# Lots behind the counts: one-hots as the stationary operand, rows as two exact 12-bit parts

## The reference

```
h = relu(layernorm(x))
x = x + sum over edges e into dst of  h[src_e] @ W0[etype_e]^T  + b0
h = relu(layernorm(x))
x = x + leaky_relu( sum over edges of norm_e * (h @ W1)[src_e] + b1, 0.2 )   # norm_e from the degrees
```

## Time and profile before

| | us |
|---|---|
| median of 3 runs | 2731.56 (2728.19 to 2732.8) |
| the profiled execution | 2727.95 |
| its span, first to last instruction | 2726.2 |
| mean granted TensorE clock | 0.903 |
| busy: PE, PEld, DVE, ACT, POOL | 2162.9, 1906.5, 1258.2, 1603.4, 1618.0 |

### The profile page before, as it was taken

How to read it: one execution, slowest core, us unless ns; L and a number is a source line. 1 busy time by engine, 2 the same in 40 slices (tenths; PEclk the granted TensorE clock), 3 DMA queues, 4 the chain that set the end, 5 groups by cost and what they waited for, 6 DMA issues and landing times.

```text
span 2726.2 us, 45144 instructions
## 1 busy us (share of the span) xinstructions
PE 2162.9 (79%) x14621; PEld 1906.5 (70%) x14621; DVE 1258.2 (46%) x3564; ACT 1603.4 (59%) x3885; POOL 1618.0 (59%) x1719
## 2 busy tenths in 40 slices
PE   1557777787787778767868889899898888898898
PEld 1446666776677677766757778787777777777776
DVE  6436545555564655555555542222222223344258
ACT  6425655666575667647656775656566656556450
POOL 2666666556665665565655556666666666666615
PEclk7678888888898898888989999999999999989899
DMA  9334444444554454445555456454445444555448
GB/s 287 104 92 121 131 118 144 123 126 129 148 162 139 124 157 132 125 122 147 153 159 157 128 149 202 142 167 135 141 126 148 132 132 127 128 137 129 123 92 107
DMA packets 366992, 378.04 MB, mean 139 GB/s; under 512 B 238627, under 2 KB 288036, under 8 KB 366628
## 3 DMA queue, kind: packets, MB, share of 16 engines
q0 software_dynamic: 85312, 221.42, 29.5%
q1 hardware_dynamic: 236772, 110.05, 15.0%
q10 hardware_dynamic: 44672, 43.64, 4.8%
HBM read 299.78 MB, written 75.19 MB: 138 GB/s over the span
## 4 chain that ended last, share of the span: by engine, by line
PE 58%; issue 13%; another core or an unknown queue 9%; DVE 9%; ACT 8%; ACTq 1%; DVEq 1%; DMA 0%; SPq 0%
PE ps_slot L1670 22%; PE ps_slot L1732 10%; PE ps_proj L1686 10%; PE ps_aux L1732 8%; PE ps_slot L1700 6%; ACT staged_f L1311 3%; ACT gap_f L1376 2%; DVE hots_f L1560 2%; DVE hots_f L1557 1%; ACT onehot_f L1384 1%; DVE acc_f L1462 1%; ACT wide_f L1369 1%; PE ps_aux L1809 1%; DVE acc_f L1600 1%
## 5 line engine op out<-in xcount | busy, mean ns | idle before, releaser
L1132 POOL DMA_INDIRECT rows_f<-table,idxT x1612 | 1531.3, 950 | 958.8 <-issue 394.6
L1670 PE MATMUL ps_slot<-onehot_f,rows_f 128*128 128x128 f32 x6448 | 952.5, 297 | 161.0 <-issue 97.5
L1670 PEld LDWEIGHTS ps_slot<-onehot_f,rows_f 128*128 128x128 f32 x6448 | 885.1, 209 | 203.3 <-issue 153.7
L1311 ACT ACTIVATE staged_f<-ps_slot 128x392 uint8<-128x392 f32 x784 | 343.8, 493 | 439.8 <-remote 270.9
L1376 ACT ACTIVATE gap_f<-iota,keyT 128x128 bf16<-128x128 bf16 x1614 | 526.8, 393 | 67.0 <-ACT staged_f L1311 33.6
L1557 DVE TENSOR_TENSOR hots_f<-ps_slot,keys_f 128x392 bf16<-128x392 bf16 x784 | 279.4, 356 | 557.7 <-remote 337.1
L1700 PE MATMUL ps_slot<-hots_f 128*128 128x98 bf16 x3136 | 246.9, 219 | 235.0 <-issue 103.4
L1384 ACT ACTIVATE onehot_f<-gap_f 128x384 f32<-128x384 bf16 x538 | 276.3, 514 | 220.0 <-remote 160.2
L1686 PE MATMUL ps_proj<-w0t,acc_f 128*128 128x256 f32 x1568 | 382.5, 393 | 25.2 <-issue 22.6
L1700 PEld LDWEIGHTS ps_slot<-hots_f 128*128 128x128 bf16 x3136 | 198.8, 117 | 284.3 <-issue 235.6
L1462 DVE TENSOR_TENSOR acc_f<-ps_slot,acc_f 128x256 f32 x538 | 227.5, 423 | 327.2 <-remote 185.5
(11 more groups left out here) (166 smaller groups left out, 970.2 us busy)
## 6 DMA issues: line engine op xcount, KB each, us to landing
rows_f<-table,idxT POOLq DMA_INDIRECT x1612
abuf_f<-counts_d SPq DMA_DIRECT2D x57, 320.0 KB
stash_f<-table SPq DMA_DIRECT2D x14, 1280.0 KB
table<-hs_f SPq DMA_DIRECT2D x48, 256.0 KB
xt_f<-in_x_dram SPq DMA_DIRECT2D x48, 128.0 KB
out_dram<-xt_f SPq DMA_DIRECT2D x48, 128.0 KB
xres<-in_x_dram SPq DMA_DIRECT2D x9, 640.0 KB, 14.0
table<-xres SPq DMA_DIRECT2D x9, 640.0 KB, 6.0
```

What stands on the lines that cost most here:

```text
L1132: eng.indirect_dma_start(rows0[:, k, c, :], None, V["table0"], bass.IndirectOffsetOnAxis(ap=idxT[:, n * LOT + c:n * LOT + c + 1], axis=0)) ...
L1311: eng.activation(staging[:, h % 2, :, (w % HSUB) * SUB:(w % HSUB + 1) * SUB], count_bank(w)[:, 0:SPAN * MW].rearrange("p (d t) -> p t d", ...
L1670: last = eng.matmul(o[:, b * W:(b + 1) * W], rows0[:, k, c, b * P:(b + 1) * P], onehot[:, n % HOTS, c, :], start=(c == 0), stop=(c == chun ...
```

## The change

For lots 322 to 530 (segments 29 to 47, the lots that start after the counts are over and stop before the last segment) the product is turned round. The one-hots are the weights, and the gathered rows move, 256 columns at a time, in f32r. To keep that exact the rows are split: DVE writes a rounded copy (`high_part`) into one of 2 new buffers, and the difference over the row itself (`low_part`). PE does 6 matmuls a lot (`sum_turned`) into banks 2 and 0 in turn; ACT copies the sums of a fill to SBUF (`take_sums`), PE turns them back with 2 fp32 transposes a lot (`turn_sums`) into bank 1, and DVE accumulates from there, one slot later than before. The planner books 0.9 us instead of 1.3 us for such a lot, the projections and chains from tile 30 on stand one slot later, and the scratch memory for gather descriptors is 8192 bytes.

```
+TURNED_FROM = 29
+HIGHS = 2
...
-        return base + (1 if t >= LATE_TILE else 3), base + (3 if t >= LATE_TILE else 7)
+        return base + (2 if t >= LATE_TILE else 3), base + (4 if t >= LATE_TILE else 7)
...
+        stored[-2] -= 2
...
-                pe += 1.3 + 0.28 * len(self.win.get(n - LEAD, ())) + (3.45 if n in self.project else 0.0)
+                pe += (0.9 if self.turned[0] <= n < self.turned[1] else 1.3) + 0.28 * len(self.win.get(n - LEAD, ())) + (3.45 if n in self.project else 0.0)
...
+            def take_sums(f):
+                until = lots_until(f)
+                width = (until - first_lot(f)) * DF
+                eng.wait_ge(s_pe, until)
+                if f >= F1 + 2:
+                    eng.wait_ge(s_turn, f - 1 - F1)
+                eng.activation(summed[:, f % 2, 0:width], ps_slot[:, SUM_BANKS[(f - F1) % 2], 0:width], ACT.Copy).then_inc(s_sum, 1)
...
             def accumulate(n, off):
-                eng.wait_ge(s_pe, lots_until(fill_of(n)))
+                if is_turned(n):
+                    eng.wait_ge(s_turn, fill_of(n) - F1 + 1)
+                else:
+                    eng.wait_ge(s_pe, lots_until(fill_of(n)))
...
+            def high_part(n):
+                k = n % RING0
+                eng.wait_ge(s_rows[k], 16 * LOT * (n // RING0 + 1))
+                if n >= N1 + HIGHS:
+                    eng.wait_ge(s_pe, n - HIGHS + 1)
+                eng.tensor_copy(rows[:, high_of(n):high_of(n) + LR].bitcast(f32r), rows[:, k * LR:(k + 1) * LR]).then_inc(s_high, 1)
+            def low_part(n):
+                k = n % RING0
+                eng.wait_ge(s_high, n - N1 + 1)
+                eng.tensor_tensor(rows[:, k * LR:(k + 1) * LR].bitcast(f32r), rows[:, k * LR:(k + 1) * LR],
+                                  rows[:, high_of(n):high_of(n) + LR], ALU.subtract).then_inc(s_low, 1)
...
+            def sum_turned(n):
+                f = fill_of(n)
+                eng.wait_ge(s_low, n - N1 + 1)
+                eng.wait_ge(s_oh, n + 1)
...
+                for c in range(LOT):
+                    for i, a in enumerate((high_of(n), k * LR)):
+                        last = eng.matmul(sum_part(n), onehot[:, n % HOTS, c, :].bitcast(f32r), rows[:, a + c * DF:a + (c + 1) * DF].bitcast(f32r),
+                                          start=(c == 0 and i == 0), stop=(c == LOT - 1 and i == 1))
+                last.then_inc(s_pe, 1)
+            def turn_sums(f):
+                eng.wait_ge(s_sum, f - F1 + 1)
+                eng.wait_ge(s_acc, first_lot(f))
+                for n in range(first_lot(f), lots_until(f)):
+                    for b in range(NB):
+                        a = (n - first_lot(f)) * DF + b * P
+                        last = eng.transpose(lot_part(n)[:, b * P:(b + 1) * P], summed[:, f % 2, a:a + P], ident[:, :])
+                last.then_inc(s_turn, 1)
...
-    nc = _bacc.Bacc("TRN2", target_bir_lowering=False, num_devices=1)
+    nc = _bacc.Bacc("TRN2", target_bir_lowering=False, num_devices=1, dynamic_dma_scratch_size=8192)
```

More of the change, by code:

```diff
@@ L678, in chain_at @@
         elif t == self.tiles - 2:
-            base = seg_start(t + 1) + 3
+            base = seg_start(t + 1) + 4
         else:
-            base = seg_start(t + 1) + (5 if t >= LATE_TILE else 9)
+            base = seg_start(t + 1) + (6 if t >= LATE_TILE else 9)
         return base, base + 1, base + 2
@@ L687, in __init__ @@
         self.tail = self.nlot + SEAM
+        self.turned = (seg_start(TURNED_FROM), seg_start(D.segs - 1))
         last_window = D.nsub * 3 // 8
         self.counts_end = FIRST_WIN + last_window + LEAD + 4
+        assert self.counts_end <= self.turned[0]
         self.win = {}
@@ L1014, in lots_until, with is_turned, lot_bank, first_lot @@
             return min(seg_start(s) + (i + 1) * LOTS_PER_BANK, seg_start(s + 1), PL.nlot)
+        N1, N2 = PL.turned
+        F1, F2 = fill_of(N1), fill_of(N2)
+        TURN_BANK = 1
+        SUM_BANKS = (COUNT_BANK, 0)
+        def is_turned(n):
+            return N1 <= n < N2
+        def lot_bank(f):
+            if f < F1:
+                return f % LOT_BANKS
+            if f < F2:
+                return TURN_BANK
+            return (f - F2) % LOT_BANKS
         def lot_part(n):
             a = (n - seg_start(seg_of(n))) % LOTS_PER_BANK * NQ * WIN
-            return ps_slot[:, fill_of(n) % LOT_BANKS, a:a + NQ * WIN]
+            return ps_slot[:, lot_bank(fill_of(n)), a:a + NQ * WIN]
+        def first_lot(f):
+            return lots_until(f - 1)
+        def sum_part(n):
+            f = fill_of(n)
+            return ps_slot[:, SUM_BANKS[(f - F1) % 2], (n - first_lot(f)) * DF:(n - first_lot(f) + 1) * DF]
+        def high_of(n):
+            return (RING0 + n % HIGHS) * LR
         weight_bank = (ps_proj, ps_aux)
@@ L1383, in build_onehot @@
                     eng.wait_ge(s_pe, n - HOTS + 1)
-                eng.activation(onehot[:, n % HOTS, :, :], gap[:, n % 2, :, :], ACT.Relu, scale=-1.0, bias=1.0).then_inc(s_oh, 1)
+                eng.activation(onehot[:, n % HOTS, :, :].bitcast(f32r), gap[:, n % 2, :, :], ACT.Relu, scale=-1.0, bias=1.0).then_inc(s_oh, 1)
+            def take_sums(f):
[5 more added lines that the diff above has]
+                eng.activation(summed[:, f % 2, 0:width], ps_slot[:, SUM_BANKS[(f - F1) % 2], 0:width], ACT.Copy).then_inc(s_sum, 1)
             def copy_weights(r):
@@ L1404, in _ @@
             for n in range(PL.slots):
+                if is_turned(n - 1) and n == lots_until(fill_of(n - 1)):
+                    take_sums(fill_of(n - 1))
                 if n + AHEAD < PL.nlot:
@@ L1418, in _ @@
                 if n < PL.nlot and s > 0:
-                    if j == 0 and s % WRAP == 0:
+                    late = 2 if s > TURNED_FROM else 0
+                    if j == late and s % WRAP == 0:
                         wrap(s)
-                    if j == 2 and s % WRAP == 0:
+                    if j == late + 2 and s % WRAP == 0:
                         eng.wait_ge(s_ring, ring_before(s))
@@ L1622, in _ @@
             for n in range(PL.slots):
[L1623 to L1630, removed]
+                if is_turned(n):
+                    high_part(n)
+                    low_part(n)
+                for ended in (n - 2, n - 1):
+                    if is_turned(ended) != (ended == n - 2):
+                        continue
+                    if 0 <= ended < PL.nlot and ended + 1 == lots_until(fill_of(ended)):
+                        for lot in range(lots_added, ended + 1):
+                            s, j = divmod(lot, LOTS)
+                            if j == 0:
+                                off = starts(s)
+                            accumulate(lot, off)
+                        lots_added = ended + 1
                 for u, half in PL.pieces.get(n - 1, ()):
@@ L1672, in sum_lot @@
                 last.then_inc(s_pe, 1)
+            def sum_turned(n):
+                f = fill_of(n)
+                eng.wait_ge(s_low, n - N1 + 1)
+                eng.wait_ge(s_oh, n + 1)
+                if f == F1:
+                    eng.wait_ge(s_ev, D.nsub)
+                elif f == F1 + 1:
+                    eng.wait_ge(s_acc, N1)
+                else:
+                    eng.wait_ge(s_sum, f - F1 - 1)
+                k = n % RING0
+                for c in range(LOT):
[11 more added lines that the diff above has]
+                last.then_inc(s_turn, 1)
             def project(t, part):
@@ L1832, in _ @@
                         dense_first_of_last(u)
+                if is_turned(n - 1) and n == lots_until(fill_of(n - 1)):
+                    turn_sums(fill_of(n - 1))
                 for k in PL.fin.get(n, ()):
```

22 lines of the change are left out of this document (17 added, 5 removed).

## The result

The changed kernel takes 2760.02 us (median of 4, 2756.39 to 2766.11) against 2729.88 before (4 runs): a ratio of 1.0126, 95% interval 1.0107 to 1.0145 (the two medians alone give 1.0110). The forecast was 2728, no change. The profiled execution is 2760.34 us, its span 2758.5.

The account below looks back on a forecast made before the run. The prediction took POOL's six-gather cycle, with PE's marks held up while POOL issues, as the bound. Its sum was 2727.95 + 209 x 0 - 3 = 2725, with 3.6 to the median 2728 us; range 2690 to 2780.

Parts of the forecast that it names:

- POOL's six-gather cycle: Late in the layer: POOL waits for PE once every six gathers; windows of 8.90 to 9.00 us set the pace.
- The tail: Behind the last lot: 49 pieces left instead of 52, 2.9 us off the tail, which PE sets.
- PE then has more idle time before its lots: Lots on PE: the saving of 0.3 us a lot becomes idle time, as PE doesn't set the pace.
- the sum with 209 x 0: Whole kernel: no gain over 209 lots, 3 us off the tail, 2725; with 3.6 to the median 2728 us.
- rival D1: Turned lots: a new loop through DVE, PE and ACT costs 0.3 us a lot; 2765 us, chance 0.24.
- Two of D1's signs: Turned lots: PE's waits for subtract or ACT's copy sum over 1 us a lot; longer POOL gaps, same gathers.
- the late marks: Late in the layer: PE's marks are held up while POOL issues; once the count wasn't passed on for 6 us.
- The moved pieces: Lots 322 to 449: 45 us of PE work moved in against 39 us saved, called even.
- the VectorE work beside the gathers: Lots on POOL: copy and subtract lengthen gathers by 0.39 us a lot, 0.78 a six-gather cycle, taken as absorbed.
- D2: Lots on POOL: longer gathers aren't absorbed; 209 x 0.39 = 82 us, giving 2810 us; chance 0.09.

Follow-up runs that it names:

- late_3: Changed kernel with the high and low parts made behind the slot's accumulates instead of ahead of them; 2624.48 us, ratio 1.1689 to the kernel before.
- ahead1: Changed kernel with DVE making the parts one slot ahead, three high buffers; 2741.97 us, ratio 1.0083 to before (repeat `ahead1_2`: 2739.67 us, 1.0072).
- before_09: Kernel before with only the plan's booking changed, 0.9 instead of 1.3 us a lot in slots 322 to 530; 2724.77 us, ratio 1.0018.
- after_13: Changed kernel with a turned lot booked at 1.3 us as before; 2749.42 us, ratio 1.0112 to the kernel before.
- before_dve_2: Kernel before plus DVE's copy and subtract on lots 322 to 530, into a spare buffer; 2733.21 us, ratio 1.0044 (`before_dve`: 2295.64 us, 1.0217).
- before_subps: Kernel before plus one subtract on each lot 322 to 530, its second operand read from PSUM; 2730.72 us, ratio 1.0041.
- before_light: Kernel before without the second of the two matmuls of each dense tile half in slots 322 to 530; 2243.25 us, ratio 0.9996.
- before_2of3: Kernel before with two gathers instead of three in each lot 322 to 530; 2235.61 us, ratio 0.9964.
- after_again: The changed kernel run again, nothing else changed; 2302.98 us, ratio 1.0252 to the kernel before.

## Why the prediction was wrong

**Right.** PE's work doesn't set the pace of lots in the second window (46 us less PE busy, no time gained); the durations of the new operations (a turned lot 0.81 us of PE from 2010.17 to 2010.98, 0.72 forecast). POOL's six-gather cycle was right for 24 runs out of 62 only.

**Right by luck.** The tail. From lot 530 to the end it is 4.0 us shorter, for the -3 forecast, but that term stood on 49 pieces left behind the last lot instead of 52. The plan leaves 52 in both kernels, only one slot sooner in the changed one, and from the last accumulate to the end it takes 98.5 us before and 98.1 after. The rest stands in lots 531 to 537, and why isn't shown.

**Wrong step.** "PE then has more idle time before its lots", and the sum with 209 x 0: I let rival D1 lose to the reading that nothing of the new chain reaches POOL's cycle. The loop of D1 did cost time, but not as D1 had it. D1 had PE wait for ScalarE's copy and had the two high buffers close the loop; in the first window PE's waits for the copy are 2.5 us and VectorE's for a free high buffer 0.2, while PE waits 63 us for the subtract, which stands behind the accumulates that wait for the turned sums. Two of D1's signs are missing: PE's waits for the subtract are 0.54 us a lot (112.2 / 209) and not over 1, and POOL's gaps aren't longer. That its 2765 us lies near the measured 2760 is luck, for it put 39 us on the loop, where a slot ahead gives back 15 to 17, and nothing on the moved pieces and the gathers. The range of 2690 to 2780 holds the time because it took D1 in. The prediction had the late marks in the earlier trace rows and listed "behind it in DVE's order stand accumulates"; it did not ask which new mark VectorE waits for ahead of the operation that PE waits for. On that hop stand the transposes' mark, two accumulates, copy and subtract, 2.6 us in `late_3` with marks on time and some 3 us more with a late one, and PE's 0.47 us of idle time a lot could not hide it.

**Two more terms put at nothing.** The moved pieces, called "even", cost 5 to 9 us, and the VectorE work beside the gathers, called absorbed, 5 us in the first window.

**The ledger of the 30.2 us in lots 322 to 450:** about 17 is the loop (`ahead1` 589.7; `ahead1_2` 15), 8 to 9 the moved pieces (`before_09`, `after_13`), 5 the VectorE work beside the gathers (`before_dve_2`: 581.7 against 576.8 in this window, of which the next gives 3 back). The three make 30 to 31, if they add, which no run tests in one kernel. These windows compare traces of different series, so each entry may be off by some us. By the ratios of whole times, of a loss of 34 us, the same three are 12 to 15, 4 to 5 and 12, of which 11 are there without any lengthened gather (`before_subps`). Not shown either: that POOL's cycle is the bound in condition A, since `before_light` and `before_2of3` ran only in B. The 62 equal cycles of 8.98 us argue for it in the kernel before; in the changed kernel most runs are no longer of six.

**D2** was the right mechanism for condition B, where POOL has no gap that could shrink: forecast 0.39 us a lot, measured 3 x 0.087 = 0.26 in `before_dve`, with the shares of copy and subtract the wrong way round.

## What to carry to other kernels

Before hiding an operation under "its engine has room", write down that engine's queue and ask for each wait in it which other engine stands behind the operations queued after it; a producer belongs ahead of any wait for the same consumer's results, and the place of two calls in one queue was worth 184 us here (607.0 against 791.0). A saving on an engine is worth nothing where another one's cycle is as long; take much of its work away in one run to see it. When a term is put at nothing, price each of its parts in a run of its own: three of them make up this loss, as far as they add. Here the gathers that began within a long VectorE operation paid for it, and a second source in SBUF was the expensive part.

## What the runs showed that was not expected

The same program runs in 2244 or 2720 us, depending on the series, with POOL's instructions equally long. In condition B a mark of PE reaches VectorE 0.75 us after the start of the transposes that give it, PE and VectorE of `after_again`:
```profile
1653.14 0.60 PE L1774 MATMUL ps_slot<-ident,summed_f 128*128 128x128 f32 x4
...
1653.89 0.42 DVE L1513 TENSOR_TENSOR acc_f<-ps_slot,acc_f 128x256 f32 x1 [3.74 <-PE ps_slot L1774]
```
In condition A the pair shown above took 3.91 us (2009.44 to 2013.35), and the gap of POOL that ends with such marks, 1.79 us every six gathers, is absent in B. The late marks that the prediction read out of the earlier trace rows are thus a property of the condition, not of the program. What POOL's 1612 gathers waited for, in the kernel before (A) and in `before_light` (B):
```profile
  issue: 394.6, 1290
  remote: 298.0, 175
  PE ps_slot L1670: 266.2, 147
```
```profile
  issue: 468.2, 1536
  PE ps_slot L1670: 31.8, 76
```
Less 0.305 us of issue for each wait, the waits sum to 466 us in A and 9 in B. The two executions are 485 us apart (2727.95 and 2242.58), so most of the difference can be laid to these gaps. What switches the condition is open.
